# A ring of seven buffers for the basis loads, and a reordered beginning

## The chip, the core and the metric

The kernel runs on one core of one Trainium2 chip. The metric is the device time in microseconds (us) of one execution; lower is better.

## The reference, cut to what matters

A graph network with 625 nodes, 20,625 edges and 512 features passes through two blocks. The change touches only the start of the first one, a two-layer relational graph convolution:

```
xn   = layernorm(x)                                  # 625 x 512
w[r] = sum over 30 bases of att[r, b] * basis[b]     # r = 0, 1; basis is 30 x 512 x 512, one set per layer
for edge e of type r:  out[row[e]] += sigmoid(xn[col[e]] . gate_w[r]) * xn[col[e]] @ w[r]
out += xn @ root + bias
```

After it come a linear attention, a mixture of experts, three graph-attention layers, another attention and another mixture, each with a residual. They are as they were.

## The kernel before, in words

Five engines run their own instruction streams and meet at semaphores. SyncE (its DMA queue is "SPq") issues nearly all loads in program order.

**The bases.** Two sets of 30 bases, 63 MB in all, are streamed from HBM in 80 loads of 768 KB (`load_basis(n)`, L2481 to L2485) into a ring of five buffers. Each buffer holds three of the 128-row chunks of bases. Five consecutive loads make one *group* of 15 chunks, and there are 16 groups: group k is loads 5k to 5k+4. TensorE combines a group with the attention coefficients in `combos(k)`: 18 matmuls of 32 columns (L442), four of which run side by side, into one bank of PSUM, `CB`. At five of the 18 (`FREES`) it raises `combo_done` by one, which frees a buffer. ScalarE (`combo_out`, even k) or VectorE (`combo_in`, odd k, L1290) then takes `CB` to the weights and raises `w_ready`; `combos(k)` waits for `w_ready >= k`, that is until the group before has been taken away.

**The edge counts.** Between the groups TensorE counts edges into matrices of node by node. The edges are cut into 24 segments of seven tiles. For segment g, VectorE and ScalarE write one-hot rows (`ends(g)`, L1278, L1281 and L1952), double-buffered: `ends(g+2)` waits until segment g is done. TensorE multiplies them (L493) and closes the segment (L495). After every odd segment g it runs `combos(g // 2 + 2)`. After every sixth segment there is a flush: ScalarE and VectorE (L1328) empty the seven banks, TensorE refills them with a constant (L483).

**The beginning.** SyncE issues the masks, edges and iota, then x (1280 KB), a constant table `cst`, loads 0 to 4, the gate weights (`load_gates`, one row of 4 KB from HBM sent to each of 125 partitions), and then loads 5 to 79, load n as soon as `combo_done >= n - 4`. TensorE runs `combos(0)`, the counts per block (`cnt`, L457), five turns of the normalized x (L430), `combos(1)`, and then the segments. VectorE runs the layernorm of x before the flags that come out of `cnt`, the copies of the turned x, and `ends(0)`, `ends(1)`. ScalarE runs `ends(0)`, the roots of the norm, `combo_out(0)`, its copies of the turned x, and `ends(1)`. `gate_rows` (L1245), run in the first five segments, is the first reader of the gate weights.

**The end of the stage.** After segment 23 ScalarE issues the load of `R1e` (root1, 1024 KB, on its own DMA queue). TensorE runs `combos(13)`, the first third of `combos(14)`, which waits for VectorE's `combo_in(13)`, then `root1(0)` (L505), which waits for R1e, then the rest of `combos(14)` and `combos(15)` between `root1(1)` to `root1(3)` and a small matmul (L524) that waits for VectorE's `many_ready`. Then `z_unit` (L548) begins, and the rest of the program follows.

Of the kernel before, what the change touches and what calls it, by code (L numbers as in the profile page):

```python
# [5 lines left out]
ALU = mybir.AluOpType  # L6
ACT = mybir.ActivationFunctionType
AX_X = mybir.AxisListType.X
# [7 lines left out]
NT = 5  # L16
# [5 lines left out]
NS = len(SEGS)  # L22
EP = 7 * NS
# [10 lines left out]
         (3, 0), (3, 1), (11, 2), (11, 3), (7, 1), (7, 2))  # L34
ORDER = (0, 4, 8, 12, 1, 5, 9, 13, 2, 6, 10, 14, 3, 11, 7)
FREES = (2, 5, 8, 11, 17)

AFTER = [g // 2 + 2 if g % 2 else None for g in range(NS)]
FLUSHES = (NS + PER - 1) // PER
# [15 lines left out]
LN_X, LN_L0, LN_F, LN_G1, LN_G2, LN_G3 = 0, 5, 10, 15, 20, 25  # L55
# [66 lines left out]
def build(nc, A, out):  # L122
    ctx = ExitStack()
    with ctx:
        def sb(name, shape, dt=F32):
            return ctx.enter_context(nc.sbuf_tensor(name, shape, dt))
# [5 lines left out]
        X = sb("X", [128, NT, 512])  # L132
# [30 lines left out]
        flags = sm[0:1, 0:3, :, :].rearrange("p k c e -> p (k c e)").rearrange("p (b g) -> p b g", b=NT)  # L163
# [12 lines left out]
        y_dram = nc.dram_tensor("y_dram", (1025, 512), F32, kind="Internal").ap()  # L176
        arena = (nc.sbuf_base + 63) // 64 * 64
        sb("slab", [128, 48320 + 16])
        AR = nc.alloc_sbuf_tensor_at("AR", [128, 48320], F32, offset=arena)

        def fr(name, off, *dims, p=128):
# [5 lines left out]
        def ar(off, *dims, p=128):  # L187
            n = 1
            for d in dims:
                n *= d  # L190
            v = AR[0:p, off:off + n]
            if len(dims) == 1:
                return v
            names = "abcdefgh"[:len(dims)]
            return v.rearrange("p (%s) -> p %s" % (" ".join(names), " ".join(names)),
                               **{k: d for k, d in zip(names, dims)})

        def sl(i, a, b, p=128):
            return PS[0:p, i * 1024 + a:i * 1024 + b]
# [32 lines left out]

        Am = ar(oA, 2, 18, 48)
        amask, att = ar(oW2, 18, 16), ar(oW2 + 512, 18, 2, 2)
        ring = ar(oR2, 5, 3, 512)
        ei = ar(oOT, 3, EP).bitcast(I32)
        ef = ar(oB + 1024, 3, EP, p=P)
        ge_ = ar(oOT + 512, NT + 1, EP, p=P)
# [157 lines left out]
        def _(te):  # L396
# [38 lines left out]
            def combos(n, a=0, b=len(PARTS)):  # L435
                l = n // 8
                pe.wait_ge(w_ready, n)
                for m, (c, j) in list(enumerate(PARTS))[a:b]:
                    at = ORDER.index(c)
                    pe.wait_ge(d_ring[at // 3], 16 * (n + 1))  # L440
                    quarter = [k for k, part in enumerate(PARTS) if part[1] == j]
                    ins = te.matmul(CB[32 * j:32 * j + 32, :], Am[:, l, m, 16 * (n % 2):16 * (n % 2) + 32],  # L442
                                    ring[:, at // 3, at % 3, :], start=m == quarter[0], stop=m == quarter[-1])
                    if m in FREES:
                        ins.then_inc(combo_done, 1)

# [15 lines left out]
            for c in range(NT):  # L462
                pe.wait_ge(xn_ready, LN_X + c + 1)
                turn(("xt", 0, c), c, XN, 4, "dve" if c % 2 else "act")
            combos(1)


            for f in psum.free:
# [683 lines left out]
        def _(ve):  # L1152
# [3 lines left out]
            def step(ins):  # L1156
                ins.then_inc(dve_step, 1)
                return steps.next()

            def full(key, less=0):  # L1160
                u = psum[key]
                dv.wait_ge(u.sem, u.full - less)
                return u.slot

            def read(u):
                for s, v in u.read:
                    dv.wait_ge(s, v)

            def ln_stats(src, F, c):
                n, w = max(1, F // 512), min(F, 512)  # L1170
                for j in range(n):
                    t = step(ve.bn_stats(st[0:P, c, 6 * j:6 * j + 6], src[0:P, c, j * w:(j + 1) * w]))
                dv.wait_ge(*t)
                ve.bn_aggr(mv[0:P, c, :], st[0:P, c, 0:6 * n]).then_inc(ln_var, 1)  # L1174
# [22 lines left out]
            def ln_scale(src, c, k):  # L1197
                dv.wait_ge(ln_sd, k)
                t = step(ve.reciprocal(rs[0:P, c:c + 1], sd[0:P, c:c + 1]))
                dv.wait_ge(*t)  # L1200
                ve.tensor_scalar(XN[0:P, c, :], src[0:P, c, :], mv[0:P, c, 0:1], rs[0:P, c:c + 1],
                                 ALU.subtract, ALU.mult).then_inc(xn_ready, 1)
# [13 lines left out]
            def turned(key, c, nk, dst, k0=0):  # L1216
                i = full(key)
                ve.tensor_copy(dst[:, k0:k0 + nk, cols(c)],
                               sl(i, 0, nk * P).rearrange("p (k n) -> p k n", k=nk)).then_inc(dve_read, 1)
# [29 lines left out]
                ins.then_inc(gl_ready, 1)  # L1249


            dv.wait_ge(d_x, 16)
            for c in range(NT):
                ln_stats(X, 512, c)
                if c:
                    ln_scale(X, c - 1, LN_X + c)
            ln_scale(X, NT - 1, LN_X + NT)
            for i, (b0, b1) in enumerate(((0, 3), (3, 5))):
                k = full(("cnt", i))
                ve.tensor_reduce(flags[0:1, b0:b1, :],  # L1260
                                 sl(k, 0, (b1 - b0) * EP, 1).rearrange("p (b g t) -> p b g t", g=NS, t=7),
                                 AX_X, ALU.add).then_inc(dve_read, 1)
            read(psum["cnt", 1])
            for b in range(NT):
                t = step(ve.tensor_scalar(flags[0:1, b, :], flags[0:1, b, :], 0.0, float(1 << b), ALU.is_gt, ALU.mult))
            dv.wait_ge(*t)
            t = step(ve.tensor_reduce(met[:, :], flags[0:1, :, :].rearrange("p b g -> p g b"), AX_X, ALU.add))
            dv.wait_ge(*t)
            ve.tensor_copy(imet[:, :], met[:, :]).then_inc(flags_ready, 1)
            for c in (1, 3):  # L1270
                turned(("xt", 0, c), c, 4, XT)


            def ends(g):
                if g > 1:
                    dv.wait_ge(seg_done, g - 1)
                for t in range(*SEGS[g]):
                    ve.tensor_scalar(oh_dst(g, t)[:, 0:N], iota[0:P, 0:N], ef[:, 1, t:t + 1], ef[:, 2, t:t + 1],  # L1278
                                     ALU.is_equal, ALU.mult).then_inc(dst_ready, 1)
                for t in by_dve(g):  # L1280
                    ve.tensor_scalar(oh_src(g, t)[:, 0:N], iota[0:P, 0:N], ef[:, 0, t:t + 1], None,  # L1281
                                     ALU.is_ge).then_inc(src_dve, 1)
# [11 lines left out]
            dv.wait_ge(d_iota, 16)  # L1294
            ends(0)
            ends(1)
            for z, o in enumerate((OFF0, OFF1)):
                before = step(ve.memset(sums[z][:, :, 0:1], -FLUSHES * o))

# [636 lines left out]
        def _(se):  # L1936
# [21 lines left out]
            def ln_root(c, k):  # L1958
                ac.wait_ge(ln_var, k)
                act(sd[0:P, c:c + 1], mv[0:P, c, 1:2], ACT.Sqrt, bias=eps[0:P, :]).then_inc(ln_sd, 1)  # L1960

            def turned(key, c, nk, dst, k0=0):
                i = full(key)
                copy(dst[:, k0:k0 + nk, cols(c)], sl(i, 0, nk * P).rearrange("p (k n) -> p k n", k=nk)).then_inc(act_read, 1)


            def ends(g):
                if g > 1:
                    ac.wait_ge(seg_done, g - 1)
                for t in by_act(g):  # L1970
                    act(oh_src(g, t)[:, 0:N], iota[0:P, 0:N], ACT.Sigmoid, bias=nsrc[:, t:t + 1],
                        scale=STEEP).then_inc(src_act, 1)
# [2 lines left out]
            ac.wait_ge(d_iota, 16)  # L1975
            ac.wait_ge(nsrc_ready, 1)
            ends(0)
            ac.wait_ge(pool_const, 1)
            for c in range(NT):
                ln_root(c, LN_X + c + 1)  # L1980


            def combo_out(k):
# [6 lines left out]
                ins.then_inc(w_ready, 1)  # L1990

            combo_out(0)
            for c in (0, 2, 4):
                turned(("xt", 0, c), c, 4, XT)
            ends(1)
            f = 0
            for g in range(NS):
                if g % PER == PER - 1 or g == NS - 1:
# [464 lines left out]
        def _(ye):  # L2463
            sp = Waits(ye)

            def full(key):
                u = psum[key]
                sp.wait_ge(u.sem, u.full)
# [11 lines left out]

            def load_basis(n):  # L2481
                r = n % 5
                if n > 4:
                    sp.wait_ge(combo_done, n - 4)
                ye.dma_start(ring[:, r, :, :], A["basis"][n]).then_inc(d_ring[r], 16)  # L2485

            ye.dma_start(X[:, :, :], A["x"].rearrange("c p f -> p c f")).then_inc(d_x, 16)
            ye.dma_start(cst[:, :], A["c_cst"]).then_inc(d_cst, 16)
            for n in range(5):
                load_basis(n)  # L2490
            def load_gates(lay, d):
                ye.dma_start(gw[lay][0:P, :, :].rearrange("p r i -> p (r i)"), A["gate_w"][lay:lay + 1, :].to_broadcast([P, 1024])).then_inc(d, 16)

            load_gates(0, d_gw0)
            for n in range(5, 80):
                load_basis(n)
                if n == 40:
                    sp.wait_ge(gl_ready, NT)
                    ye.dma_start(bias1, A["bias1"]).then_inc(d_bias, 16)
                    ye.dma_start(bias2, row(A["L0_gnn_bias2"]).to_broadcast([P, 512])).then_inc(d_bias2, 16)  # L2500
# [161 lines left out]
```

## Time and profile before

| | |
|---|---|
| time, median of 3 runs | 1013.95 us (1012.62 to 1014.72) |
| span of the profiled execution, first to last instruction | 1014.3 us |
| TensorE busy | 945.3 us (93%) |
| VectorE, ScalarE, GpSimd busy | 556.8, 400.6, 109.6 us |
| HBM read | 120.4 MB |

No separate device time is kept for the profiled execution, so its span stands for it; it lies 0.35 us above the median of the runs. Times in the profile are from the start of the span. An arrow gives what ended an engine's idle time. A matmul's busy time is modelled. The share of the DMA engines is a mean over the core's 16.

### The profile page before, as it was taken

Reading aid. Unit: us, or ns where it says so; the run is one execution under the profiler, and the core shown is the slowest. Engines: PE = TensorE matmul, PEld = TensorE weight load, DVE = VectorE, ACT = ScalarE, POOL = GpSimd, SP = SyncE. Lnnn points to the kernel's source line nnn. Section 1 sums busy time; section 2 is a strip of 40 time slices with the busy share of each in tenths; the row PEclk is TensorE's granted clock in tenths of the full one; section 3 lists DMA queues with packets and bytes.
Section 4 is the critical chain, followed back from the end, with each engine's and each line's share of the span. In section 5 each row is a group of like instructions: output and inputs, shape, how many; then the busy total and the mean of one; then the engine's idle time right before and its main releaser. Section 6 shows DMA issues by size and latency. Waiting matters only on the chain. (4 is left out here: it accounts for less than half of the span.)

```text
span 1014.3 us, 12428 instructions
## 1 busy us (share of the span) xinstructions
PE 945.3 (93%) x4724; PEld 612.8 (60%) x4724; DVE 556.8 (55%) x1176; ACT 400.6 (39%) x670; POOL 109.6 (11%) x98
## 2 busy tenths in 40 slices
PE   3789889799999999999999899989999899999998
PEld 1245445257454476458775655889998644445885
DVE  5588887742227541334212772498777643558871
ACT  3467775331111211111111332468786553423550
POOL 0000000000020023100002000144331000022300
PEclk9899999799999999998999999999999999999899
DMA  8888988852000102016595400513101300230001
GB/s 305 281 341 332 336 325 343 321 196 90 0 14 6 51 3 83 1 46 233 199 319 187 172 0 1 172 43 84 43 1 44 123 1 3 87 83 0 1 2 50
DMA packets 53039, 124.87 MB, mean 123 GB/s; under 512 B 5408, under 2 KB 19492, under 8 KB 52963
## 3 DMA queue, kind: packets, MB, share of 16 engines
q1 hardware_dynamic: 51314, 121.46, 33.9%
q0 software_dynamic: 1120, 1.29, 0.5%
q8 instruction: 56, 0.92, 0.4%
q10 hardware_dynamic: 528, 1.05, 0.3%
q14 instruction: 21, 0.16, 0.0%
HBM read 120.40 MB, written 3.38 MB: 122 GB/s over the span
## 5 line engine op out<-in xcount | busy, mean ns | idle before, releaser
L409 PE MATMUL PS<-AR 128*125 128x512 f32 (+9 forms) x1394 | 394.0, 440 | 9.0 <-issue 1.9
L409 PEld LDWEIGHTS PS<-AR 128*128 128x128 f32 (+3 forms) x1394 | 212.5, 194 | 169.0 <-issue 161.9
L442 PE MATMUL PS<-AR 128*32 128x512 f32 x576 | 88.2, 628 | 35.4 <-DMA AR<-in_basis 34.4
L1949 ACT ACTIVATE AR<-PS 128x500 f32<-128x500 f32 (+6 forms) x73 | 41.9, 578 | 167.3 <-PE PS L409 81.5
L1952 ACT ACTIVATE AR<-iota,AR 125x625 f16<-125x625 f16 x119 | 86.1, 810 | 39.1 <-PE PS L495 38.9
L442 PEld LDWEIGHTS PS<-AR 128*32 128x32 f32 x576 | 19.4, 111 | 91.0 <-issue 56.2
L1278 DVE TENSOR_SCALAR AR<-iota,AR 125x625 f16<-125x625 f16 x165 | 60.5, 442 | 17.6 <-PE PS L495 17.6
L493 PE MATMUL PS<-AR 125*125 125x512 f16 (+9 forms) x425 | 61.2, 302 | 3.5 <-issue 3.4
L493 PEld LDWEIGHTS PS<-AR 125*125 125x125 f16 x425 | 46.2, 142 | 21.7 <-issue 12.3
L2447 POOL TENSOR_TENSOR whl<-AR,whh 128x512 fp32r<-128x512 f32 x32 | 47.8, 1513 | 89.8 <-ACT whh L1949 89.8
L1797 DVE TENSOR_TENSOR HMl<-AR,HMh 128x626 fp32r<-128x626 f32 x64 | 51.3, 841 | 4.6 <-ACT HMh L1949 4.6
L1949 ACT ACTIVATE HMh<-AR 128x626 fp32r<-128x626 f32 x64 | 43.2, 729 | 13.7 <-DVE AR L1792 13.7
L1952 ACT ACTIVATE sd<-mv,eps 125x1 f32<-125x1 f32 x35 | 10.3, 297 | 93.8 <-DVE mv L1174 86.6
L548 PE MATMUL PS<-Dr,GXh 125*128 125x314 f32 (+1 forms) x160 | 46.7, 310 | 0.0
L548 PE MATMUL PS<-Dr,GXl 125*128 125x314 f32 (+1 forms) x160 | 46.2, 307 | 0.0
L1952 ACT ACTIVATE AR<-PS,bh 128x626 f32<-128x626 f32 (+1 forms) x48 | 35.8, 780 | 18.4 <-PE PS L409 18.2
L409 PE MATMUL PS<-HMh,whh 128*128 128x314 f32 (+1 forms) x128 | 39.8, 311 | 1.8 <-ACT AR L1952 1.6
L1388 DVE TENSOR_SCALAR AR<-PS 125x512 f32<-125x512 f32 (+1 forms) x18 | 13.4, 742 | 50.8 <-PE PS L409 50.8
L409 PE MATMUL PS<-x1h,whh 128*128 128x314 f32 (+1 forms) x128 | 40.1, 313 | 1.1 <-DVE AR L1792 0.8
L409 PE MATMUL PS<-x1h,whl 128*128 128x314 f32 (+1 forms) x128 | 40.1, 313 | 0.0
L409 PE MATMUL PS<-x1l,whh 128*128 128x314 f32 (+1 forms) x128 | 39.4, 308 | 0.0
L409 PE MATMUL PS<-HMl,whh 128*128 128x314 f32 (+1 forms) x128 | 39.3, 307 | 0.0
(318 smaller groups left out, 1479.1 us busy)
## 6 DMA issues: line engine op xcount, KB each, us to landing
AR<-in_basis SPq DMA_DIRECT2D x80, 768.0 KB, 8.3
AR<-in_L_ffn_W SPq DMA_DIRECT2D x20, 1024.0 KB, 7.8
AR<-in_L_gnn_Wh SPq DMA_DIRECT2D x8, 512.0 KB, 4.0
AR<-in_L_gnn_Wh SPq DMA_DIRECT2D x16, 256.0 KB, 4.7
AR<-in_L_mix_W_qkv SPq DMA_DIRECT2D x1, 3072.0 KB, 11.3
AR<-in_L_gnn_root SPq DMA_DIRECT2D x2, 1024.0 KB, 14.7
y_dram<-AR SPq DMA_DIRECT2D x8, 256.0 KB, 8.1
AR<-in_WkvT SPq DMA_DIRECT2D x1, 2048.0 KB, 8.6
```

What stands on the lines that cost most here:

```text
L409: ins = te.matmul(o, l, r, start=start and i == 0, stop=stop and i == len(pairs) - 1)
L442: ins = te.matmul(CB[32 * j:32 * j + 32, :], Am[:, l, m, 16 * (n % 2):16 * (n % 2) + 32], ring[:, at // 3, at % 3, :], start=m == quarter[ ...
L493: te.matmul(PS[0:P, p0:p1], oh_dst(g, t)[:, cols(b)], oh_src(g, t)[:, p0 - b * N:p1 - b * N], start=False, stop=False, skip_group_check=True)
L548: ins = te.matmul(o, w, Dr[r][0:P, d, a:b], **z)
L1278: ve.tensor_scalar(oh_dst(g, t)[:, 0:N], iota[0:P, 0:N], ef[:, 1, t:t + 1], ef[:, 2, t:t + 1], ALU.is_equal, ALU.mult).then_inc(dst_ready, 1)
L1388: ve.tensor_scalar(t, i, 0.0, None, ALU.min).then_inc(phi_min, 1)
L1797: ve.tensor_tensor(HMl[q][:, f, :], tmp[f], f32(HMh[q][:, f, :]), ALU.subtract).then_inc(hm_lo, 1)
L1949: return se.activation(o, i, ACT.Copy, scale=scale)
L1952: return se.activation(o, i, f, bias=bias, scale=scale)
L2447: ge.tensor_tensor(lo[:, ks], v, f32(hi[:, ks]), ALU.subtract).then_inc(pool_wl, 1)
```

## The change

- The ring has seven buffers; the two new ones (`spare`) lie outside the old arena. Load n goes to buffer n mod 7 and waits for `combo_done >= n - 6`. There are still five landing semaphores, used in turn, so load n also waits until load n-5 has landed: at most five loads are in flight.
- SyncE issues `cst` and loads 0 to 4 ahead of x, and loads 5 to 9 ahead of the gate weights.
- VectorE runs `ends(0)` and `ends(1)`, then the flags, then the norm, then its copies. ScalarE runs `ends(0)` and `ends(1)`, `combo_out(0)`, and then the roots with its copies among them.
- TensorE runs `combos(1)` in three parts: after turn 0, after turn 2, and after turn 4.
- The memory set aside for the descriptors of DMAs that GpSimd issues is set to 4096 bytes per partition (`dynamic_dma_scratch_size`); it was the default. GpSimd issues such DMAs at L2431 only, five gathers in the mixture of experts.

```diff
+SLOTS = 7
+        spare = sb("spare", [128, 3072])
-        ring = ar(oR2, 5, 3, 512)
+        ring = [ar(oR2 + 1536 * i, 3, 512) for i in range(5)] + [
+            spare[:, 1536 * i:1536 * i + 1536].rearrange("p (c n) -> p c n", c=3) for i in range(2)]
...
+                    held = ring[(5 * n + at // 3) % SLOTS]
...
             for c in range(NT):
                 pe.wait_ge(xn_ready, LN_X + c + 1)
                 turn(("xt", 0, c), c, XN, 4, "dve" if c % 2 else "act")
-            combos(1)
+                if c in (0, 2):
+                    combos(1, 3 * c, 3 * c + 6)
+            combos(1, 12)
...
             def load_basis(n):
                 r = n % 5
-                if n > 4:
-                    sp.wait_ge(combo_done, n - 4)
-                ye.dma_start(ring[:, r, :, :], A["basis"][n]).then_inc(d_ring[r], 16)
-
-            ye.dma_start(X[:, :, :], A["x"].rearrange("c p f -> p c f")).then_inc(d_x, 16)
+                if n >= 5:
+                    sp.wait_ge(d_ring[r], 16 * (n // 5))
+                if n >= SLOTS:
+                    sp.wait_ge(combo_done, n - SLOTS + 1)
+                ye.dma_start(ring[n % SLOTS], A["basis"][n]).then_inc(d_ring[r], 16)
+
             ye.dma_start(cst[:, :], A["c_cst"]).then_inc(d_cst, 16)
             for n in range(5):
                 load_basis(n)
+            ye.dma_start(X[:, :, :], A["x"].rearrange("c p f -> p c f")).then_inc(d_x, 16)
+            for n in range(5, 10):
+                load_basis(n)
...
             load_gates(0, d_gw0)
-            for n in range(5, 80):
+            for n in range(10, 80):
                 load_basis(n)
...
-    nc = bacc.Bacc("TRN2", target_bir_lowering=False, num_devices=1)
+    nc = bacc.Bacc("TRN2", target_bir_lowering=False, num_devices=1, dynamic_dma_scratch_size=4096)
```

On VectorE the calls move from `norm(x); flags; copies 1, 3; ends(0); ends(1)` to `ends(0); ends(1); flags; norm(x); copies 1, 3`. On ScalarE they move from `ends(0); roots; combo_out(0); copies 0, 2, 4; ends(1)` to `ends(0); ends(1); combo_out(0); roots with copies 0, 2; copy 4`.

## Rows read from the trace of the kernel before

**Rows 1.** The page: the span; the waits of TensorE (us, times, longest).

```profile
span 1014.3 us, 12428 instructions
...
PE PS L442 <- DMA AR<-in_basis: 34.4, 14, 13.6
```

**Rows 2.** Timeline of the start, SyncE's queue: start, duration, what, how often.

```profile
2.63 0.43 SPq L2487 DMA_DIRECT2D X<-in_x  x1
...
7.00 0.38 SPq L2492 DMA_DIRECT2D AR<-in_gate_w  x1
```

**Rows 3.** Timeline of the start, TensorE: combos(0) and combos(1) following the landings.

```profile
13.59 4.73 PE L442 MATMUL PS<-AR 128*32 128x512 f32 x18 [13.59 <-DMA AR<-in_basis]
...
15.38 0.20 PEld L442 LDWEIGHTS PS<-AR 128*32 128x32 f32 x6 [1.59 <-DMA AR<-in_basis]
...
17.26 0.15 PEld L442 LDWEIGHTS PS<-AR 128*32 128x32 f32 x6 [1.69 <-DMA AR<-in_basis]
...
21.27 1.07 PE L442 MATMUL PS<-AR 128*32 128x512 f32 x8 [1.06 <-DMA AR<-in_basis]
...
32.32 6.62 PE L442 MATMUL PS<-AR 128*32 128x512 f32 x24 [5.46 <-DMA AR<-in_basis]
...
39.76 1.92 PE L442 MATMUL PS<-AR 128*32 128x512 f32 x12 [0.82 <-DMA AR<-in_basis]
```

**Rows 4.** Timeline of the start, VectorE: the norm's first and last step.

```profile
10.99 0.69 DVE L1172 BATCH_NORM_STATS2 st<-X 125x6 f32<-125x512 f32 x1 [2.46 <-DMA X<-in_x]
...
18.81 0.55 DVE L1201 TENSOR_SCALAR AR<-X,mv,rs 125x512 f32<-125x512 f32 x1
```

**Rows 5.** Timeline, first segments: the constant, and combos(2) after segments 0 and 1.

```profile
41.60 1.72 PE L483 MATMUL PS<-AR 1*125 1x512 f16 x7
...
47.30 4.49 PE L442 MATMUL PS<-AR 128*32 128x512 f32 x36
```

**Rows 6.** SyncE's queue: issue of load 14, then of loads 15 to 19.

```profile
41.71 0.33 SPq L2485 DMA_DIRECT2D AR<-in_basis  x1
...
48.41 3.75 SPq L2485 DMA_DIRECT2D AR<-in_basis  x5
```

**Rows 7.** DMA issues of load 14, then of load 15: the last column is us to landing.

```profile
AR<-in_basis SPq DMA_DIRECT2D x1, 768.0 KB, 7.4
...
AR<-in_basis SPq DMA_DIRECT2D x1, 768.0 KB, 4.3
```

**Rows 8.** Stretch 40 to 123 us: busy time of each engine, TensorE's clock, DMA share, GB/s.

```profile
40.00:123.00 83.00, 73.80 (x511) 39.05 (x503) 66.84 (x173) 58.91 (x86) 0.00 (x0) 0.98 0.87 329
```

**Rows 9.** Timeline of TensorE: last loads of groups 8 and 12.

```profile
123.25 1.92 PE L442 MATMUL PS<-AR 128*32 128x512 f32 x12 [0.84 <-DMA AR<-in_basis]
...
167.13 3.56 PE L442 MATMUL PS<-AR 128*32 128x512 f32 x24
171.52 1.92 PE L442 MATMUL PS<-AR 128*32 128x512 f32 x12 [0.82 <-DMA AR<-in_basis]
```

**Rows 10.** Timeline of the stage's end: R1e's issue, combo_in(13), root1(0), root1(1), first z.

```profile
177.63 0.42 ACTq L2001 DMA_DIRECT2D AR<-in_L_gnn_root  x1
...
184.43 1.40 DVE L1290 SCALAR_TENSOR_TENSOR AR<-PS,cst,AR 128x512 f32<-128x512 f32 x2
...
192.19 6.66 PE L505 MATMUL PS<-AR 128*125 128x512 f32 x8 [1.12 <-DMA AR<-in_L_gnn_root]
...
200.62 3.70 PE L505 MATMUL PS<-AR 128*125 128x512 f32 x8
...
218.75 0.41 PE L548 MATMUL PS<-Dr,GXh 125*128 125x314 f32 x1
```

**Rows 11.** Stretch 190 to 200 us, columns as in Rows 8.

```profile
190.00:200.00 10.00, 8.88 (x24) 2.89 (x20) 9.05 (x24) 0.00 (x0) 0.00 (x0) 0.59 0.67 276
```

**Rows 12.** The gathers, by line: duration of an issue in ns, and us to landing.

```profile
L2431 POOL DMA_INDIRECT AR<-y_dram,gidx x5: 1211/1214/1393, 543.8 to 550.1; - x5
...
DMA to landing us min/median/max: 5.4/5.8/6.0
```

More of the change, by code:

```diff
@@ L440, in combos @@
                     pe.wait_ge(d_ring[at // 3], 16 * (n + 1))
+                    held = ring[(5 * n + at // 3) % SLOTS]
                     quarter = [k for k, part in enumerate(PARTS) if part[1] == j]
                     ins = te.matmul(CB[32 * j:32 * j + 32, :], Am[:, l, m, 16 * (n % 2):16 * (n % 2) + 32],
-                                    ring[:, at // 3, at % 3, :], start=m == quarter[0], stop=m == quarter[-1])
+                                    held[:, at % 3, :], start=m == quarter[0], stop=m == quarter[-1])
                     if m in FREES:
@@ L1249, in gate_rows @@
                 ins.then_inc(gl_ready, 1)
[L1252 to L1271, printed above, removed]
             def ends(g):
@@ L1296, in _ @@
             ends(1)
+            for i, (b0, b1) in enumerate(((0, 3), (3, 5))):
+                k = full(("cnt", i))
+                ve.tensor_reduce(flags[0:1, b0:b1, :],
+                                 sl(k, 0, (b1 - b0) * EP, 1).rearrange("p (b g t) -> p b g t", g=NS, t=7),
+                                 AX_X, ALU.add).then_inc(dve_read, 1)
+            read(psum["cnt", 1])
+            for b in range(NT):
+                t = step(ve.tensor_scalar(flags[0:1, b, :], flags[0:1, b, :], 0.0, float(1 << b), ALU.is_gt, ALU.mult))
+            dv.wait_ge(*t)
+            t = step(ve.tensor_reduce(met[:, :], flags[0:1, :, :].rearrange("p b g -> p g b"), AX_X, ALU.add))
+            dv.wait_ge(*t)
+            ve.tensor_copy(imet[:, :], met[:, :]).then_inc(flags_ready, 1)
+            dv.wait_ge(d_x, 16)
+            for c in range(NT):
+                ln_stats(X, 512, c)
+                if c:
+                    ln_scale(X, c - 1, LN_X + c)
+            ln_scale(X, NT - 1, LN_X + NT)
+            for c in (1, 3):
+                turned(("xt", 0, c), c, 4, XT)
             for z, o in enumerate((OFF0, OFF1)):
@@ L1977, in _ @@
             ends(0)
-            ac.wait_ge(pool_const, 1)
-            for c in range(NT):
-                ln_root(c, LN_X + c + 1)
+            ends(1)
             def combo_out(k):
@@ L1992, in _ @@
             combo_out(0)
-            for c in (0, 2, 4):
-                turned(("xt", 0, c), c, 4, XT)
-            ends(1)
+            ac.wait_ge(pool_const, 1)
+            for c in range(NT):
+                ln_root(c, LN_X + c + 1)
+                if c in (2, 4):
+                    turned(("xt", 0, c - 2), c - 2, 4, XT)
+            turned(("xt", 0, 4), 4, 4, XT)
             f = 0
```

## The prediction

> **What bounds the kernel now.** I read the page first. TensorE is busy 93% of the span, and the one thing that it waits for in earnest is the landing of the bases: 34.4 us in 14 waits [rows 1]. All of them lie in the first 219 us, so I read that stretch alone; after it nothing is edited except the gathers' descriptor memory. The timeline of the start shows combos(0) and combos(1) fed load by load: TensorE resumes at 15.38 and 17.26, so a load lands every 1.88 us (768 KB, 418 GB/s) [rows 3]. Then there is a hole: load 4 is used at 21.27, load 5 not until 32.32 [rows 3]. What stands between the two in SyncE's queue is the gate load, issued at 7.00 [rows 2].
>
> From 40 to 123 us the DMA engines are busy 87% of the time, TensorE 73.8 of 83 us, VectorE 66.8 [rows 8]. No resource is full; the parties wait in turns. The queue's timeline says why: load 14 is issued at 41.71, the next only at 48.41 [rows 6], because all five buffers are full until combos(2) begins at 47.30 [rows 5]. A stream that stopped so needs 4.3 us from issue to landing to come back [rows 7].
>
> **The beginning: the order of the loads.** x (1280 KB) moves behind load 4: it takes 1280/768 x 1.88 = 3.1 us of stream, so load 0 lands at 13.6 - 3.1 = 10.5 [rows 3], load 4 at 18.0, x at 21.1. Loads 5 to 9 need no later buffer than combos(0) frees, are issued by then, and follow x at 1.88 each: load 9 at 30.5 instead of 39.8 [rows 3], 9.2 us earlier.
>
> Then come the gates. Before, load 5 followed load 4 by 11.05 us instead of 1.88 [rows 3]: the gates hold the stream up by 9.2 us. They have only changed place. Load 14 thus lands at 30.5 + 9.2 + 5 x 1.88 = 49.1. Before it landed at 41.71 + 7.4 = 49.1 [rows 6, 7]. **The reordering wins 9.2 us and meets the same 9.2 us again before group 2.** The rows only bound this price: at least the gates' 500 KB as a part of 768 (1.2 us), at most 9.2. The same broadcast stands among the same loads, so I take 9.2.
>
> The Trainium skill weighs in here. "DMA: Bandwidth & Descriptors", section "Why a DMA increments its semaphore by 16 and not by 1", says that a DMA runs on the largest number of engines up to 16 that divides its outer dimension: 125 rows go to five. With its section "Where 436 GB/s comes from" (16 ports, 435 GB/s), five ports would carry 512 KB in an estimated 3.8 us. The trace shows 9.2, more than twice that; by the page, group 2 would be 5.4 us earlier and the total near 1000. The measured hole decides.
>
> **The beginning: the engines.** The norm takes from 10.99 to 19.36, 8.4 us [rows 4]. Now it starts after x (21.1) and after the flags, which need the counts behind combos(0) (20) and some 3 us of VectorE: about 23. It ends at 31.5; with the last turn and copies segment 0's constant is written at about 35.5 instead of 41.60 [rows 5], and combos(2) could start at 35.5 + (47.30 - 41.60) = 41.2. It waits for load 14 until 49.1, so this part has 8 us of cover at the start and 3 at the end, and I price it at nothing. The same cover hides TensorE waiting at turn 0 with combos(1) queued behind it, and VectorE waiting at the flags with the norm behind it. The gates' data have moved by about 40 (30.5 + 9.2); the first gate_rows comes after ends(2), about 41. After load 14 there is 1.9 us of combos [rows 3]: combos(2) ends at 51.0 instead of 51.8.
>
> **Seven buffers.** From load 15 on the stream needs no pause. Before, it paused three times up to 123 us. Load 15 landed at 48.41 + 4.3 = 52.7, 3.6 after load 14 [rows 6, 7], 1.7 more than 1.88; at the starts of groups 5 and 6 the same sum gives 2.0 and 2.1. Together 5.8 us. From above: 13% of 83 us is 10.8 us of DMA idle time [rows 8], but that is a mean over engines, and part of it is not a full ring. I take 5.8. A full ring needs combos(k) to begin after load 5k+6 has landed; up to group 8 each combos waits for its own last load, 5k+4, so the ring never fills. The extra wait, load n behind the landing of n-5, costs nothing: five loads are 9.4 us of stream, a lone landing 4.3 [rows 7]. combos(8) then has its last load at 123.25 - 5.8 = 117.4 [rows 9].
>
> Behind it the loads no longer rule; TensorE, VectorE and the flushes do, as before. Up to segment 23 there is one more loss to loads: combos(12) began at 167.13, got its last load at 171.52 and ended at 173.4 [rows 9]; an unbroken 4.49 us [rows 5] ends at 171.6. That 1.8 goes. Segment 23 ends 5.8 + 1.8 = 7.6 us earlier.
>
> **The stage's end.** R1e is issued when segment 23 is done and used 14.6 us later, at 192.19 [rows 10]. combos(14)'s first part no longer waits for loads, but it cannot start before combo_in(13) ends (185.8 [rows 10]), and root1(0) still waits for R1e, which shares the engines with basis loads. Alone it would need 1.33 x 1.88 + 2.4 = 4.9 us; TensorE could be there at 187.5, 4.7 us sooner. At the stop the clock falls: 0.59 of full in 190 to 200 [rows 11], and root1(0) takes 6.66 against root1(1)'s 3.70 [rows 10], 3.0 us more. So the end gives between 0 and 7.7 us; loads are as dense then as before, so I take 1.5. From the first z_unit (218.75 [rows 10]) the rest moves rigidly.
>
> **The sum.** 5.8 + 1.8 + 1.5 = 9.1 us: a span of 1005.2, and 0.35 less for the median of the runs: about 1005.
>
> **The gathers.** Less descriptor memory could make GpSimd wait between them; the rows show 1.21 us per issue and 5.8 to landing [rows 12]. Between nothing and four waits of 4.3 us after the first gather, 17 us; five gathers of 125 rows are little work for the queue, so I take nothing. The Trainium skill ("SBUF — State Buffer", "SBUF size: 192, 224, or 256?") gives this memory as 16 KiB by default; no run shows what a quarter holds.
>
> **Rivals.**
> - *The forecast*: the gates keep their price, pauses go. 1001 to 1009. Chance 0.60.
> - *The gates cost little in their new place.* For: while they run the rate halves for all engines, which is odd for 500 KB, and fewer broadcast rows may collide now; the page's 3.8 us. Then the loads run ahead of TensorE: 6.1 us from the earlier segment 0, plus the losses to loads up to segment 23 (some 12 of the 34.4 us), of which VectorE, busy 66.8 of 83 us, lets about 8 through, plus 1.5: 998. Against: the hole of 11 us is plain. Chance 0.18.
> - *VectorE takes the loads' place.* In the stretch it has only 16 us of slack, and its one-hots, flush and gate rows hang on segment ends. If landings come sooner but VectorE does not, 2 to 3 us remain: 1011 to 1013. Chance 0.12, a third of it within 0.2%.
> - *The gathers wait* for one another's landings. The price is up to 17 us and decides above 9.1: 1014 - 9 + 17 = 1022, slower. Against: GpSimd's queue is nearly empty. Chance 0.05.
> - Other slower cases, such as TensorE waiting long enough at the turns for a slow clock to carry on: 0.05.
>
> **How the numbers follow.** 0.2% (2 us) is what a measurement of this kernel can tell from no change. Faster: 0.60 + 0.18 + 0.08 = 0.86; within: 0.05; slower: 0.09. The range takes in the bound from DMA idle time (another 5 us less) and part of the third case: 996 to 1011.
>
> **What would show it.** Right: combos(0) starts near 10.5; the first constant near 35.5; combos(2) paced by loads and ending near 51; another hole of 9 us between loads 9 and 10; combos(8) ending near 119; segment 23's R1e issue near 170; the first z_unit near 209.5. Wrong: combos(2) not waiting for loads (the gates are cheap, a better time); combos(4) to combos(8) without load waits and yet no earlier (VectorE); DMA share still 0.87; gathers more than 1.6 us apart.

## The result, and the profile after

The changed kernel takes 1005.3 us, median of 20 runs (1000.8 to 1008.9). The kernel before, run beside it, takes 1009.6 (1004.2 to 1015.4). The ratio is 0.9952, with a 95% interval of 0.9937 to 0.9967: 3 to 6 us faster. The forecast was about 1005, and a change of 9.1 us. **The time came true and the change, 4.3 us, is half of the forecast.** Two errors cancelled, which is luck: the sum started 4.3 us too high and took off 4.8 us too much. One run of the kernel before, beside the second group below, took 1588.9 us at a granted clock of 0.557, and no ratio or spread here counts it.

The profile after, first the page's span and then the waits of TensorE up to 260 us (us, times, longest), to be read against [rows 1]. In the changed kernel combos is L446, the turns L433, a segment L499 and its close L501, the constant L489, root1 L511 and the first z L554; on VectorE the one-hots are L1262, combo_in L1274 and the flush L1332:

```profile
span 1004.1 us, 12501 instructions
...
PE PS L446 <- DMA AR<-in_basis: 12.2, 5, 9.8
PE PS L433 <- DVE AR L1207: 5.2, 1, 5.2
...
PE PS L446 <- DVE AR L1274: 3.8, 1, 3.8
PE PS L511 <- DMA AR<-in_L_gnn_root: 2.4, 1, 2.4
```

The waits for bases fell from 34.4 us in 14 waits to 12.2 in 5 (and one of 0.3 for a load in `spare`), of which 9.8 are the start itself. Waits for VectorE came in, 5.2 us at the first turn and 3.8 at `combos(14)`; before, no row of them was above 0.8 us (1.5 in a second profile).

SyncE's queue at the start, against [rows 2]:

```profile
3.09 2.74 SPq L2492 DMA_DIRECT2D AR<-in_basis  x5
5.87 0.65 SPq L2497 DMA_DIRECT2D X<-in_x  x1
...
17.67 0.37 SPq L2501 DMA_DIRECT2D AR<-in_gate_w  x1
22.51 2.21 SPq L2492 DMA_DIRECT2D AR<-in_basis  x2
```

TensorE's timeline of the start, against [rows 3] and [rows 5]:

```profile
9.84 4.88 PE L446 MATMUL PS<-AR 128*32 128x512 f32 x18 [9.84 <-DMA AR<-in_basis]
...
24.95 1.07 PE L433 MATMUL PS<-cst,AR 125*128 125x125 f32 x4 [5.17 <-DVE AR L1207]
25.94 3.63 PE L446 MATMUL PS<-spare,AR 128*32 128x512 f32 x12
...
34.03 1.92 PE L446 MATMUL PS<-AR 128*32 128x512 f32 x12
35.87 1.72 PE L489 MATMUL PS<-AR 1*125 1x512 f16 x7
...
43.88 2.12 PE L446 MATMUL PS<-AR 128*32 128x512 f32 x10 [0.27 <-issue]
...
49.27 1.92 PE L446 MATMUL PS<-AR 128*32 128x512 f32 x12 [0.55 <-DMA AR<-in_basis]
```

Load 0 is used at 9.84 instead of 13.59, segment 0's constant is written at 35.87 instead of 41.60, and group 2 still waits for load 14 at 49.27. The DMA issues of load 9 (issued at 17.3), load 10 (22.51) and load 14 (32.34), with the us to landing last:

```profile
AR<-in_basis SPq DMA_DIRECT2D x1, 768.0 KB, 14.0
...
AR<-in_basis SPq DMA_DIRECT2D x1, 768.0 KB, 19.2
...
AR<-in_basis SPq DMA_DIRECT2D x1, 768.0 KB, 16.9
```

Load 9 lands at 31.3, load 10 at 41.7, load 14 at 49.2. The hole of 10.4 us stands where the gates now stand. The stretch 40 to 123 us, against [rows 8] (the last three columns are TensorE's granted clock, the DMA share and GB/s):

```profile
40.00:123.00 83.00, 74.18 (x507) 39.98 (x506) 68.08 (x176) 61.12 (x88) 0.00 (x0) 0.94 0.90 342
```

The granted clock is 0.94 here, before it was 0.98; more on this below. The end of the stage, timelines, against [rows 10], and the gathers, against [rows 12]:

```profile
177.45 1.40 DVE L1274 SCALAR_TENSOR_TENSOR AR<-PS,cst,AR 128x512 f32<-128x512 f32 x2
...
178.91 3.63 PE L446 MATMUL PS<-AR 128*32 128x512 f32 x12 [3.79 <-DVE AR L1274]
...
184.96 5.17 PE L511 MATMUL PS<-AR 128*125 128x512 f32 x8 [2.42 <-DMA AR<-in_L_gnn_root]
...
210.02 0.41 PE L554 MATMUL PS<-Dr,GXh 125*128 125x314 f32 x1
...
DMA to landing us min/median/max: 5.5/5.7/5.9
```

The first z comes at 210.0 instead of 218.8; from there to the end are 794.1 us, before 795.5 (795.1 in its second profile). Nearly all of the gain is in the first stage.

### The profile page after: what moved, and what is told of

The parts are those of the page before. It is cut to its first block and busy times, and to the rows that moved or that the text cites. A ratio compares the mean times of both kernels' runs of the same rounds, so it can differ in the third digit from the quotient of the medians.

```text
span 1004.1 us, 12501 instructions
## 1 busy us (share of the span) xinstructions
PE 942.9 (94%) x4724; PEld 613.2 (61%) x4724; DVE 557.7 (56%) x1176; ACT 401.1 (40%) x670; POOL 109.3 (11%) x98
## 5 line engine op out<-in xcount | busy, mean ns | idle before, releaser
L446 PE MATMUL PS<-AR 128*32 128x512 f32 x420 | 68.9, 648 | 16.6 <-DMA AR<-in_basis 11.9
L1262 DVE TENSOR_SCALAR AR<-iota,AR 125x625 f16<-125x625 f16 x165 | 60.5, 444 | 19.1 <-PE PS L501 19.0
L499 PE MATMUL PS<-AR 125*125 125x512 f16 (+9 forms) x425 | 61.2, 302 | 2.8 <-issue 1.8
L499 PEld LDWEIGHTS PS<-AR 125*125 125x125 f16 x425 | 46.2, 142 | 21.2 <-issue 11.7
L446 PEld LDWEIGHTS PS<-AR 128*32 128x32 f32 x420 | 15.5, 114 | 53.7 <-issue 37.9
L554 PE MATMUL PS<-Dr,GXh 125*128 125x314 f32 (+1 forms) x160 | 46.7, 310 | 0.0
L554 PE MATMUL PS<-Dr,GXl 125*128 125x314 f32 (+1 forms) x160 | 46.2, 307 | 0.0
L412 PE MATMUL PS<-HMh,whh 128*128 128x314 f32 (+1 forms) x128 | 39.8, 311 | 1.8 <-ACT AR L1956 1.6
L412 PE MATMUL PS<-x1l,whh 128*128 128x314 f32 (+1 forms) x128 | 39.4, 308 | 0.0
```

The source lines that it names most:

```text
L412: ins = te.matmul(o, l, r, start=start and i == 0, stop=stop and i == len(pairs) - 1)
L499: te.matmul(PS[0:P, p0:p1], oh_dst(g, t)[:, cols(b)], oh_src(g, t)[:, p0 - b * N:p1 - b * N], start=False, stop=False, skip_group_check=True)
L554: ins = te.matmul(o, w, Dr[r][0:P, d, a:b], **z)
```

## The experiments

Twelve runs were made, two of them repeats, in three groups (the four up to scratch_only; the next four; the last four), each with a profile and beside runs of the kernel before, whose medians were 1011.2, 1011.3 and 1009.8 us. The table gives the median, the ratio to the kernel before of its own group with its interval, and from the one profiled execution of each: the span, load 14's landing, and the first z. The landings come from the DMA issues.

| kernel | median us | ratio | span | load 14 | first z |
|---|---|---|---|---|---|
| before, first profile | 1009.6 | | 1014.3 | 49.1 | 218.8 |
| changed kernel | 1005.3 | 0.9952 (0.9937 to 0.9967) | 1004.1 | 49.2 | 210.0 |
| before_again | 1011.1 | 1.0002 (0.9983 to 1.0021) | 1010.8 | 48.6 | 215.7 |
| order_only | 1007.6 | 0.9959 (0.9936 to 0.9982) | 1005.5 | 48.6 | 211.4 |
| ring_only | 1005.9 | 0.9943 (0.9918 to 0.9968) | 1007.9 | 48.5 | 212.5 |
| scratch_only | 1009.5 | 0.9993 (0.9970 to 1.0017) | 1008.6 | 47.5 | 214.5 |
| gates_128 | 1000.7 | 0.9900 (0.9870 to 0.9930) | 999.7 | 42.1 | 205.3 |
| gates_125_own_rows | 1004.1 | 0.9923 (0.9896 to 0.9950) | 1002.4 | 49.2 | 208.3 |
| gates_128_own_rows | 1004.0 | 0.9929 (0.9899 to 0.9958) | 997.0 | 41.0 | 201.8 |
| group1_whole | 1003.7 | 0.9929 (0.9901 to 0.9956) | 1001.2 | 46.7 | 207.1 |
| after_again | 1004.9 | 0.9961 (0.9940 to 0.9981) | 1000.7 | 46.4 | 206.4 |
| old_gates_128 | 1003.9 | 0.9942 (0.9923 to 0.9961) | 1003.9 | 42.7 | 209.4 |
| gates_bias_128 | 1003.3 | 0.9930 (0.9909 to 0.9952) | 1001.5 | 42.0 | 206.2 |
| gates_bias_128_whole | 1003.1 | 0.9932 (0.9906 to 0.9959) | 1004.3 | 44.0 | 209.1 |

The intervals are 0.15 to 0.3% wide to either side. Neighbours in the table can't be told apart by them. The landings of one kernel differ by up to 2.8 us between its two profiles (46.4 and 49.2), so only larger differences of them are read.

### Where a profile of the kernel before lies among its runs

No edit.

> The kernel before, unchanged, run as if it were a change. The profiled execution of before has a span of 1014.3 us, and the 20 timed runs have a median of 1009.6; the profiled run of after has a device time 1.8 us above its span. If a program's device time is its span plus 1.8 us, the first profile of before was of an execution of 1016 us, some 6 us slower than the median, and a second profile should have a span near 1008. The ratio should be 1.000 within 0.3%. If the second span is again near 1014, the profiler itself adds the difference.

The ratio is 1.0002. The second profile's span and granted clock, from the view of the cores:

```profile
core 0: 1010.8 us, clock 0.981
```

That execution had a device time of 1012.6 us, again 1.8 above its span. The expectation of a span near 1008 failed by 3 us, but the relation held: the first profile of before, 1014.3, belongs to a device time of about 1016.1, worked out with the 1.8, which is 6.5 us above the median of 1009.6. The 0.35 us "above the median" of the prediction compared a span with device times. And a single profiled execution can lie 2 to 5 us off its kernel's median: ring_only's was its slowest run (1009.7 for 1005.9), after_again's its fastest (1002.5 for 1004.9), and so was that of gates_128_own_rows (998.9 for 1004.0).

### The order alone, the ring alone

order_only is the changed kernel with one edit:

```diff
-SLOTS = 7
+SLOTS = 5
```

> The changed kernel with a ring of five: the reordered beginning alone. My account (the 9.2 us won ahead of load 9 are met again in the gates' hole): combos(0) still starts near 9.8, but loads 5 to 9 need only buffers freed by combos(0), the hole of 10 us stands behind load 9, load 14 lands near 49 and combos(2) ends near 51; the pauses of the ring come back, so the time is that of before, ratio 0.998 to 1.001. Rival, that the early start is what helps: ratio near 0.995, that of the whole change.

Here I was wrong. The landing of load 14 is as expected (48.6), and the time is nevertheless better, 0.9959. TensorE's timeline from segment 1 on:

```profile
38.59 2.10 PE L499 MATMUL PS<-AR 125*125 125x512 f16 x14
40.53 0.18 PE L501 MATMUL PS<-zer 125*125 125x8 f16 x1
41.22 1.06 PE L446 MATMUL PS<-AR 128*32 128x512 f32 x6 [0.51 <-DMA AR<-in_basis]
43.00 1.06 PE L446 MATMUL PS<-AR 128*32 128x512 f32 x6 [0.72 <-DMA AR<-in_basis]
...
48.66 1.92 PE L446 MATMUL PS<-AR 128*32 128x512 f32 x12 [0.83 <-DMA AR<-in_basis]
```

and SyncE's queue from 40 us on:

```profile
42.37 17.42 SPq L2492 DMA_DIRECT2D AR<-in_basis  x9
```

TensorE is ready 6 us earlier than before and takes each load as it lands, so load 15 is issued at 42.37 instead of 48.41 [rows 6] and lands 1.9 us behind load 14, without a pause. The ring of five is not too small there; it was full only because its reader came late. Further on it still is: loads 20 and 30 land 2.5 and 2.2 us late.

ring_only is the kernel before with the ring's edits alone: `SLOTS = 7`, `spare`, `held`, and `load_basis` as in the change, and the descriptor memory that makes room.

> The kernel before with seven buffers and the wait on the landing of load n-5, in the old order. My account: nearly the whole gain, ratio 0.994 to 0.997; the pause before load 15 goes, load 14 lands near 49. Loads 5 and 6 can be issued before combos(0) frees anything, which changes nothing, as they queue behind the gates. Rival (the order matters): ratio 0.998 to 1.001.

It came out as expected, 0.9943. Load 15 lands 1.9 us behind load 14 here too, this time because the buffer was free. **Each half wins about what the whole wins** (0.9959 and 0.9943 against 0.9952 and 0.9961; two gains that add would give 0.990). Both remove the pause before load 15, but that is only 1.4 to 1.7 us of the 3.6 and 5.3 that the medians won. More lies behind it, between loads 14 and 44. A *pause* here is what a load lands later than 1.88 us behind the last one, where it was issued after a wait and at most one load was in flight; the rest is all other lateness beyond 30 x 1.88 = 56.4 us:

| profile | load 14 to load 44, us | pauses (loads) | rest |
|---|---|---|---|
| before | 74.1 | 5.8 (15, 25, 30) | 11.9 |
| before_again | 72.9 | 5.8 (15, 25, 30) | 10.7 |
| scratch_only | 73.6 | 7.2 (15, 25, 30) | 10.0 |
| order_only | 70.0 | 4.7 (20, 30) | 8.9 |
| ring_only | 67.9 | 1.6 (32) | 10.0 |
| changed kernel | 68.7 | 4.1 (27, 32) | 8.3 |
| after_again | 65.7 | 3.5 (32) | 5.8 |

The three kernels with the old order and five buffers need 73 to 74 us, each half alone 68 to 70, both 66 to 69. What the halves share beyond load 15 isn't shown.

### The descriptor memory

```diff
-    nc = bacc.Bacc("TRN2", target_bir_lowering=False, num_devices=1)
+    nc = bacc.Bacc("TRN2", target_bir_lowering=False, num_devices=1, dynamic_dma_scratch_size=4096)
```

> The kernel before with 4096 bytes per partition for the descriptors of GpSimd's DMAs, nothing else. My account: the five gathers are still issued 1.5 us apart and land in 5.8 us; ratio 1.000 within 0.2%. Rival (the gathers wait for one another): gathers more than 5 us apart, ratio up to 1.017.

The gathers by line:

```profile
L2431 POOL DMA_INDIRECT AR<-y_dram,gidx x5: 1211/1211/1396, 538.2 to 544.4; - x5
...
DMA to landing us min/median/max: 5.4/5.6/5.9
```

Five issues in 6.2 us and 5.6 us to landing are as in [rows 12]. The ratio is 0.9993: no cost is seen, at most 0.2%, and that rival falls.

### What the gates' hole is

Three kernels change the changed kernel's first load of gates only. gates_128 has three rows more, which nobody reads:

```diff
-                ye.dma_start(gw[lay][0:P, :, :]..., A["gate_w"][lay:lay + 1, :].to_broadcast([P, 1024]))
+                rows = P if lay else 128
+                ye.dma_start(gw[lay][0:rows, :, :]..., A["gate_w"][lay:lay + 1, :].to_broadcast([rows, 1024]))
```

> The changed kernel with the first load of gate weights sent to 128 partitions instead of 125 (three rows more, never read), still all from one row of 4 KB in HBM. Two theories of the hole of 10.4 us between loads 9 and 10. (a) Few engines: a DMA with 125 rows runs on five of the 16 engines (the Trainium skill, DMA: Bandwidth & Descriptors, Why a DMA increments its semaphore by 16 and not by 1), and the loads behind it wait for these five; 128 rows run on all 16 and the hole shrinks from 10.4 to about 3.2 us (1.9 for load 10 and 1.3 for 512 KB). (b) One row of HBM read over and over by all is slow, whoever reads it: the hole stays above 6 us. By (a) combos(2) waits for no load and the time falls by 3 to 6 us against the changed kernel (ratio to before 0.990 to 0.993).

gates_125_own_rows reads 125 distinct rows, laid out in HBM beforehand; gates_128_own_rows reads 128:

```diff
+    a["gate_rows"] = np.tile(a["gate_w"][0:1], (128, 1))
...
+                src = A["gate_w"][lay:lay + 1, :].to_broadcast([P, 1024]) if lay else A["gate_rows"][0:125, :]
```

> The changed kernel with the gate weights laid out in HBM once per partition (125 rows of their own), still 125 rows. By (a), few engines, the hole stays at 9 to 10.4 us or falls to about 5.7 (1.9 and 512 KB over five engines at the rate that a load has on 16, 3.8 us). By (b), one row read by all, it shrinks to 5.7 us or less and the basis loads beside it keep their full rate. The difference between this and the kernel with 128 rows splits the hole into its two parts.

> Both at once: 128 rows, each with its own copy in HBM. The hole is 3.2 us by either theory. Load 14 lands near 42 instead of 49. Then TensorE and VectorE set the pace from the start: segment 0's constant stays at 35.9, combos(2) runs at once after segment 1 and ends near 46 instead of 51. The gain against the changed kernel is at most 5 us at that point, and less at the end if VectorE takes over: ratio to before 0.989 to 0.994. If the gates' hole were not what held the beginning back, the ratio would be 0.995 like the changed kernel's.

Load 10's row among the DMA issues, first of gates_128 (issued at 22.86), then of gates_125_own_rows (issued at 22.55):

```profile
AR<-in_basis SPq DMA_DIRECT2D x1, 768.0 KB, 11.7
```

```profile
AR<-in_basis SPq DMA_DIRECT2D x1, 768.0 KB, 19.2
```

Load 10 lands at 34.5 against 41.7. Its distance to load 9 is 3.15 us with 128 rows, from one row in HBM or from 128 alike, and 10.2 us with 125 rows of their own. Over all profiles the hole is 3.1 to 3.2 us with 128 partitions (five profiles) and 6.4 to 11.0 with 125 (nine). So the count of partitions makes the hole, and the rereading of one row of HBM, my other theory, makes none of it. The Trainium skill's rule ("DMA: Bandwidth & Descriptors", section "Why a DMA increments its semaphore by 16 and not by 1") is the largest number of engines up to 16 that divides the outer dimension, so 5 for 125 and 16 for 128. The trace agrees: of the gate load's 4 KB packets more than five are in flight in under 10% of the time that they take in any of the nine profiles, and 12 to 19 at the peak in the five. The estimate of 3.8 us from the Trainium skill's port figure (section "Where 436 GB/s comes from") is too low: 4.6 to 9.1 us beyond the load's own 1.9 were measured.

The packets (the trace has the start, length and size of each) also show where the excess goes. The other engines are not idle in the hole. The stretch 31 to 36 of the changed kernel, then 28 to 31 of gates_128, both in the middle of the gate load (columns as above):

```profile
31.00:36.00 5.00, 5.00 (x36) 1.76 (x35) 1.03 (x5) 2.44 (x3) 0.00 (x0) 1.00 1.02 212
```

```profile
28.00:31.00 3.00, 3.00 (x16) 1.14 (x10) 2.38 (x8) 0.29 (x1) 0.00 (x0) 0.64 1.03 419
```

All 16 are busy in both, and with 125 partitions they move half as much. A 4 KB packet of the gates takes 252 to 306 ns there on average, with 128 partitions 161 to 162; a 6 KB packet of the basis loads beside them takes 352 to 396 ns, with 128 partitions 238 to 239; ahead of the gates it is 234 to 238 in all. So the load on few engines slows the packets of all of them. Why it does is open.

With the hole gone TensorE no longer waits for loads at group 2; the timeline of gates_128:

```profile
42.45 0.22 PE L501 MATMUL PS<-zer 125*125 125x8 f16 x1 [1.00 <-issue]
42.95 1.48 PE L446 MATMUL PS<-AR 128*32 128x512 f32 x10 [0.28 <-issue]
...
45.52 1.92 PE L446 MATMUL PS<-AR 128*32 128x512 f32 x12
```

combos(2) ends at 47.4 instead of 51.2. At the end the gain isn't shown: the intervals of gates_128 and gates_128_own_rows (0.9900, 0.9929) overlap those of the two kernels of their group with the hole (gates_125_own_rows 0.9923, group1_whole 0.9929). The 7 us at the landing of load 14 are worth something from nothing to about 5 us.

### The one edit on the old kernel

old_gates_128 is the kernel before, old order, ring of five, with the edit of gates_128.

> The kernel before, old order and ring of five, with one edit: the first load of gate weights goes to 128 partitions instead of 125. If the hole behind that load is due to five engines carrying it, it shrinks here as it did in the changed kernel: load 5 lands near 24.5 instead of 31.5, load 9 near 32, combos(1) is no longer late and segment 0's constant comes near 34 instead of 41. The one edit then wins as much as the whole change: ratio 0.992 to 0.996. Rival: the ring of five pauses before group 2 instead and eats it, ratio 0.998 or more.

TensorE's timeline:

```profile
26.59 2.76 PE L442 MATMUL PS<-AR 128*32 128x512 f32 x18
...
31.76 1.92 PE L442 MATMUL PS<-AR 128*32 128x512 f32 x12 [0.82 <-DMA AR<-in_basis]
33.60 1.72 PE L483 MATMUL PS<-AR 1*125 1x512 f16 x7
```

Load 5 lands at 24.2 and load 9 at 31.7; segment 0's constant is written at 33.6, earlier than in the changed kernel; in the old order the norm runs while combos(0) does. The ratio is 0.9942, in the same group as after_again's 0.9961. **Three unused rows in one load win at least as much as the reordering and the larger ring together.**

### Group 1 among the turns, and the bias

group1_whole is the changed kernel with:

```diff
-                if c in (0, 2):
-                    combos(1, 3 * c, 3 * c + 6)
-            combos(1, 12)
+            combos(1)
```

> The changed kernel with combos(1) in one piece after the last turn. By my account the engines' part of the beginning has 8 us of cover behind load 14, so this costs at most 3 us at segment 0's constant (near 39 instead of 35.9) and nothing at combos(2), which still waits for load 14 at 49: ratio as the changed kernel's, 0.995. It also frees the buffers of group 1 later, which delays loads 12 to 14 by issue but not by landing, as the gates' hole stands ahead of them. Rival (combining group 1 among the turns is part of the gain): 2 to 3 us slower than the changed kernel.

Segment 0's constant comes at 37.9 instead of 35.9, and the time is not worse: 0.9929 against 0.9952 and 0.9961. The split of combos(1) wins nothing that these runs can see.

gates_bias_128 has 128 partitions for the gates and for bias2, whose load stands ahead of load 41:

```diff
-                    ye.dma_start(bias2, row(A["L0_gnn_bias2"]).to_broadcast([P, 512])).then_inc(d_bias2, 16)
+                    ye.dma_start(ar(oB + 512, 512), row(A["L0_gnn_bias2"]).to_broadcast([128, 512])).then_inc(d_bias2, 16)
```

> The changed kernel with 128 partitions for the gate weights and for bias2 too, whose load stands before load 41 (in the changed kernel load 41 lands 5.65 us after load 40). The gap falls to about 2.6 us, so 3 us of stream are won at load 41. With the gates on 128 partitions TensorE waits there for loads 41 to 44; the gain over that kernel (ratio 0.990) is 1 to 3 us: ratio 0.987 to 0.990. If VectorE sets the pace there, nothing.

Load 41 lands 3.0 us behind load 40 (2.8 in the next kernel), in the changed kernel 5.65 (112.3 against 106.7), and 3.3 to 6.7 over the twelve profiles with 125 partitions: probably the same effect in a second place. The time, 0.9930, is below after_again's 0.9961 of the same group, but the intervals overlap, and it is not below gates_128's 0.9900 of another; the further gain of 1 to 3 us was not seen.

> The same with combos(1) in one piece after the last turn. With the gates' hole gone, load 14 lands near 42 and the cover of 8 us is down to about 1, so now the place of combos(1) can count: segment 0's constant near 38 instead of 35.7, so up to 2 us slower than the version with combos(1) among the turns. If equal, combining the second group among the turns is worth nothing even there.

It is equal, 0.9932, as its second alternative has it, although here most of the cover was gone (load 14 at 44.0) and segment 0's constant came at 37.6 for 36.2.

after_again ran the changed kernel in this last group.

> The changed kernel again, so that it stands beside the kernels of this group on the same chip. Ratio to before 0.995 within 0.3%; the first z near 209 to 211.

The ratio repeated, 0.9961; the first z, 206.4, came earlier than expected.

## Why the prediction was right, and where it was not

**The base of the sum: wrong.** 1014.3 less 0.35 is 1013.95, the median of three runs. All three are among the four slowest of the 20 runs; the median of the 20 is 1009.6, 4.3 us lower, and on that base the sum gives 1009.6 - 9.1 = 1000.5. The 0.35 also compared a span with device times: by its device time the profiled execution, from which all rows are read, was 6.5 us slow. By the two profiles the change is 10.2 us, by the runs 4.3; only the runs count.

**The size of the change: too large, and its mechanism half wrong, in the term "seven buffers".** The forecast took pauses of 5.8 us out of the stream between loads 14 and 44. Counted in the same way (the table above) they fell from 5.8 and 5.8 us in the two profiles of before to 4.1 and 3.5 in the two of after, and to 1.6 in ring_only. In the changed kernel about two thirds of them moved and did not go. Load 31 is issued at 73.91 and load 32 only at 84.40, and it lands 4.2 us later:

```profile
73.91 0.33 SPq L2492 DMA_DIRECT2D AR<-in_basis  x1
...
84.40 0.33 SPq L2492 DMA_DIRECT2D AR<-in_basis  x1
```

The sentence that failed is "up to group 8 each combos waits for its own last load, 5k+4, so the ring never fills". TensorE's waits between 50 and 115 us:

```profile
PE PS L501 <- issue: 2.7, 2, 1.6
PE PS L489 <- DVE AR L1332: 1.6, 6, 0.3
PE PS L499 <- DVE AR L1262: 0.6, 1, 0.6
PE PS L446 <- DMA spare<-in_basis: 0.3, 1, 0.3
```

It waits 0.3 us for loads there (0.6 in the second profile), in the kernel before 6.0 (3.2). From these waits I conclude, without an experiment, that the round of segments, flush and one-hots sets the pace from group 5 on, and the ring fills behind it. The third rival ("VectorE takes the loads' place"), which I gave 0.12, describes this stretch; the forecast describes the ones around it. Even so load 44 lands 68.7 and 65.7 us after load 14, against 74.1 and 72.9, since the lateness outside the pauses fell too (8.3 and 5.8 us, against 11.9 and 10.7). The traces don't show why, and it stays open. So the 5.8 us were there in the profiles, by a way that I had not described; in the medians the whole change is 4.3 us, less than this term alone. That the first profile was of a slow execution doesn't explain it: the pauses are as long in before_again and longer in scratch_only, at 1012.6 and 1010.4 us.

**The granted clock: not in the sum, and a possible part of the answer.** In after_again's group the mean clock of the runs is 0.977 in the changed kernel (12 runs) and 0.983 in the kernel before (30). Within one kernel the time goes with it: a straight line through those 30 runs falls by 6 us per 0.01. Runs at an equal clock, 0.976 to 0.980, have medians of 1013.0 (before, 8 runs) and 1004.8 (changed, 7 runs), 8 us apart and near the 9.1 of the sum. All kernels with seven buffers have means of 0.975 to 0.981, all with five 0.981 to 0.983. And between 40 and 123 us, where the first profile of the changed kernel has 0.94, the second has 0.98, as before, and goes from load 14 to load 44 in 3.0 us less. So the change may save about 8 us and lose 3 to 4 to a lower clock. These are estimates from runs that differ by themselves; no experiment set the clock, and why it is lower is open.

**The reordering wins nothing: wrong as said, right in its reason.** The 9.2 us are won (8.4 at load 9) and met again: load 9 at 31.3 for 30.5 forecast, load 14 at 49.2 for 49.1, combos(2)'s end at 51.2 for 51.0, segment 0's constant at 35.87 for 35.5, segment 23's R1e issue at 170.65 for about 170, the first z at 210.0 for 209.5. But order_only, at 0.9959 where nothing was forecast, shows that an earlier reader empties the ring and so removes a pause that the sum had given to the seven buffers alone. The two parts share one gain. The 1.8 us of combos(12) went as said: it runs unbroken from 162.09 to 166.58.

**The gates' price: right, and its cause found in part.** Beyond the load's own 1.88 us the hole is 8.5 us for 9.2 forecast, but only 4.6 in the second profile, near the 3.8 estimated from the Trainium skill's port figure; it varies by itself (8.6 to 11.0 us in four profiles with the old order). The rival "the gates cost little in their new place" falls, since combos(2) waits for load 14 in both profiles.

**The stage's end: about right.** From R1e's issue to the first z there were 41.1 us, now 39.4 (first profiles), and 39.8, then 40.8 (second profiles). The forecast 1.5 us can't be told from nothing. root1(0) still waits for R1e, 14.3 us after its issue for 14.6.

**The gathers: right**, nothing.

## What to carry to other kernels

Ask of every load how many engines carry it, and what is queued behind it: 125 partitions instead of 128 held a stream of 768 KB loads up by three to eight us, and three unused rows took that away; on the old kernel that alone was worth 0.6%. A larger ring and an earlier reader work on the same stretch, so their gains must not be added, and a pause that goes can come back where the next limit lets the ring fill. Before a sum is made on one profiled execution, place its device time among many runs: here a span 0.35 us from the median of three belonged to a run 6.5 us slow, and the three were slow themselves. Compare the granted clock of the runs before a gain is called small.

## What the runs showed of the hardware that was not expected

- A load to 125 partitions (4 KB each) delayed the next load's landing to 6.4 to 11.0 us behind the last one's, to 128 partitions to 3.1 to 3.2; the rereading of one row of HBM did not matter (10.2 us with rows of their own).
- In that hole the DMA engines are all busy (share 1.02) and move 212 GB/s instead of 419; 6 KB packets of other loads take 352 to 396 ns instead of 234 to 239.
- In 30 runs of the kernel before, the mean granted clock ranges from 0.976 to 0.990, and the time falls by about 6 us per 0.01 of it.
- The device time is 1.8 us above the span in every run that gives both.
- Executions of one and the same kernel spread by 8 to 13 us in 1010 where 20 or more were timed, by 3 to 11 where it was 6 to 12.
